# Silu of four input projections: one ScalarE silu each, in pairs, in place of tanh, identity and a VectorE product

## The reference

```python
x_and_res = x @ Wi + bi                       # x: layer-normed input, 128 -> 4 x 128 columns
xs, res = jnp.split(x_and_res, [D_INNER], axis=-1)
xs = jax.nn.silu(xs)
x_dbl = xs @ Wx + bx                          # d_raw, B_sel, C_sel
delta = jax.nn.softplus(d_raw @ Wdt + bdt)
h = exp(delta_t[..., None] * A) * h + delta_t[..., None] * B_t[:, None, :] * x_t[..., None]   # 512 steps
y = C_t * jnp.sum(h, axis=-1)
y = (y + xs * Dp) * jax.nn.silu(res)
out = layernorm(y @ Wo + bo + x)
```

## Time and profile before

| | us |
|---|---|
| median of 3 runs | 2027.9 (2025.98 to 2030.78) |
| the profiled execution: its time | 2027.03 |
| its span, from first to last instruction | 2025.2 |
| DVE busy | 1693.6 (84%) |
| POOL busy | 1519.6 (75%) |
| PE busy | 1377.8 (68%) |
| ACT busy | 1136.7 (56%) |
| mean granted TensorE clock | 0.84 of full speed |

### The profile page before, as it was taken

How to read it: one execution, slowest core, us unless ns; L and a number is a source line. 1 busy time by engine, 2 the same in 40 slices (tenths; PEclk the granted TensorE clock), 3 DMA queues, 4 the chain that set the end, 5 groups by cost and what they waited for, 6 DMA issues and landing times. The chain is left out here.

```text
span 2025.2 us, 23533 instructions
## 1 busy us (share of the span) xinstructions
PE 1377.8 (68%) x5800; PEld 592.7 (29%) x5800; DVE 1693.6 (84%) x2401; ACT 1136.7 (56%) x2176; POOL 1519.6 (75%) x885
## 2 busy tenths in 40 slices
PE   2134448768676878767786768767786768668857
PEld 0000013324232333323332333314332333224424
DVE  1699989999898889898898988998898989896433
ACT  1256755656567555755666655765566656544323
POOL 1198998878987798877987788877987789874111
PEclk9555558879898889878898898879798899879869
DMA  3500320032000400022000310022000310000000
GB/s 90 194 1 0 117 83 0 6 110 81 11 1 25 170 13 0 21 97 77 11 0 24 126 46 11 0 87 108 11 0 24 112 60 6 1 5 1 6 0 6
DMA packets 34153, 88.25 MB, mean 44 GB/s; under 512 B 5363, under 2 KB 20598, under 8 KB 25846
## 3 DMA queue, kind: packets, MB, share of 16 engines
q1 hardware_dynamic: 34038, 87.12, 12.0%
HBM read 75.58 MB, written 11.53 MB: 43 GB/s over the span
## 5 line engine op out<-in xcount | busy, mean ns | idle before, releaser
L815 POOL TENSOR_TENSOR w<-ur,br 128x1024 f32<-128x1024 f32 x512 | 1199.1, 2357 | 237.7 <-DVE h L1114 219.2
L1114 DVE TENSOR_TENSOR_SCAN h<-da,w 128x512 f32<-128x512 f32 x1024 | 1204.4, 1207 | 74.1 <-ACT da L711 28.1
L711 ACT ACTIVATE da<-dr,al 128x511 f32<-128x511 f32 x1024 | 691.1, 692 | 250.1 <-DVE h L1114 225.1
L558 PE MATMUL ys<-h,wsum 128*32 128x512 f32 x2048 | 333.5, 729 | 194.9 <-DVE h L1114 165.9
L499 PE MATMUL bankH<-nT,w 128*128 128x512 f32 x512 | 307.7, 685 | 112.2 <-DVE sq L1044 112.1
L661 ACT ACTIVATE tq<-bankH 128x512 f32<-128x512 f32 x256 | 153.0, 598 | 378.7 <-PE bankH L499 378.7
L499 PE MATMUL bankG<-nT,w 128*128 128x512 f32 x512 | 295.5, 661 | 60.7 <-DVE aq L1053 60.4
L512 PEld LDWEIGHTS bankY<-w,aq 128*128 128x128 f32 x2048 | 263.7, 204 | 114.0 <-issue 64.2
L761 POOL TENSOR_TENSOR x<-x,yk 128x512 f32<-128x512 f32 x128 | 162.5, 1269 | 169.5 <-ACT yk L674 168.8
L512 PE MATMUL bankY<-w,aq 128*128 128x128 f32 x2048 | 270.4, 288 | 27.1 <-DVE aq L1053 19.7
L1044 DVE SCALAR_TENSOR_TENSOR sq<-tq,bankH 128x512 f32<-128x512 f32 x256 | 170.4, 666 | 100.7 <-ACT tq L661 100.5
(11 more groups left out here) (175 smaller groups left out, 837.0 us busy)
## 6 DMA issues: line engine op xcount, KB each, us to landing
br<-b_rows SPq DMA_DIRECT2D x32, 1024.0 KB, 7.8
dr<-d_rows SPq DMA_DIRECT2D x16, 1024.0 KB, 5.3
ur<-u_rows SPq DMA_DIRECT2D x16, 1024.0 KB, 7.9
d_rows<-vh SPq DMA_DIRECT2D x16, 256.0 KB
u_rows<-th SPq DMA_DIRECT2D x16, 256.0 KB
xnew<-in_L_attn_a_x_dram SPq DMA_DIRECT2D x8, 256.0 KB, 3.2
w<-in_L_ffn_W_dram SPq DMA_DIRECT2D x2, 1024.0 KB, 7.0
x<-in_L_attn_a_x_dram SPq DMA_DIRECT2D x8, 256.0 KB, 7.6
```

The lines of the kernel that those rows point to most:

```text
L558: ins = nc.tensor.matmul(ys[32 * q:32 * q + 32, :], wsum[:, :], h[:, (2 * group + q // 2) % H_RING, q % 2, :], start=(n == 0), stop=(n == ...
L711: A(da[duo % D_RING][:, k % 2, 1:L], dr[:, half, q, 1:L], ACT.Exp, scale=nega[:, QUADS * half + q, n:n + 1]).then_inc(decay_ready, 1)
L815: G.tensor_tensor(w[:, duo % W_RING, :, :], ur[:, half, q:q + 2, :], br[:, n:n + 1, :].to_broadcast([128, 2, L]), ALU.mult).then_inc(produ ...
L1114: V.tensor_tensor_scan(h[:, duo % H_RING, k % 2, :], da[duo % D_RING][:, k % 2, :], w[:, duo % W_RING, k % 2, :], 0.0, ALU.mult, ALU.add). ...
```

## The change

ACT writes the silu of a projection straight from the bank, with the bias, into `xs` or `sres`, and frees the bank. Line 622 and DVE's line 970 go, and so does the halving of the bias at the start (line 849). Two projections are taken together: ACT waits for `in0` and `in1` (then for `in2` and `in3`), at the later one's slot plus 3. The waits for the buffers move along: those that guarded `xs` and `sres` on DVE now stand on ACT, and the wait for `steps_stored`, which guarded `th`, stands ahead of line 637. In the table, `in2`, `in3`, `stepsB`, `C0`, `C1` and `dt0` move by one to three slots, and `C0` and `C1` change banks. `copy_out` (line 584) waits for the filled bank, runs one ACTIVATE and frees the bank.

```diff
--- before.py
+++ after.py
@@ -80,8 +80,8 @@
     (S5_AT + 14, "post", "H", "s5"), (S5_AT + 17, "post", "Y", "s5t"),
     (MOE_AT[2] - 2, "post", "Y", "x3T"), (MOE_AT[2], "post", "Y", "lg2"),
 ] + [(PRE_AT + _n, "pre", _b, _name) for _n, _b, _name in (
-    (0, "H", "xnT"), (2, "G", "in0"), (3, "H", "in1"), (6, "G", "in2"), (7, "H", "in3"), (10, "G", "stepsB"),
-    (13, "G", "C0"), (14, "H", "C1"), (16, "G", "dt0"), (24, "H", "dt1"))]
+    (0, "H", "xnT"), (2, "G", "in0"), (3, "H", "in1"), (8, "G", "in2"), (9, "H", "in3"), (12, "G", "stepsB"),
+    (14, "H", "C0"), (15, "G", "C1"), (17, "G", "dt0"), (24, "H", "dt1"))]
 for _m in MOE_AT:
     for _j in range(2 * E):
         PE_STEPS.append((tile_slot(_m, _j), "late" if is_late_tile(_m, _j) else "post", "H", f"h{_m}_{_j}"))
@@ -197,7 +197,7 @@
         ident = sb("ident", [128, 128])
         wsum = sb("wsum", [128, 32])
         rev = sb("rev", [128, E])
-        hbi = sb("hbi", [128, 4]); bxs = sb("bxs", [128, 1]); bxc = sb("bxc", [128, 2])
+        bis = sb("bis", [128, 4]); bxs = sb("bxs", [128, 1]); bxc = sb("bxc", [128, 2])
         bdts = sb("bdts", [128, 2]); dps_ = sb("dps_", [128, 2]); bcs = sb("bcs", [128, 3, D])
         one_col = sb("one_col", [128, 1]); mhalf = sb("mhalf", [128, TT]); minus = sb("minus", [128, TT]); eps = sb("eps", [128, TT])
         al = sb("al", [128, 2 * QUADS, PER_QUAD]); nega = al
@@ -250,7 +250,7 @@
         stats_ready = [sem(f"stats_ready{k}") for k in range(5)]; moments_ready = [sem(f"moments_ready{k}") for k in range(5)]
         rstd_ready = [sem(f"rstd_ready{k}") for k in range(5)]; normed = [sem(f"normed{k}") for k in range(5)]
 
-        tanh_ready = sem("tanh_ready"); biased_ready = sem("biased_ready"); abs_ready = sem("abs_ready"); relu_ready = sem("relu_ready"); exp_ready = sem("exp_ready"); log_ready = sem("log_ready")
+        abs_ready = sem("abs_ready"); relu_ready = sem("relu_ready"); exp_ready = sem("exp_ready"); log_ready = sem("log_ready")
         inputs_ready = sem("inputs_ready")
 
         sums_gated = sem("sums_gated"); scaled_ready = sem("scaled_ready"); x1_ready = sem("x1_ready"); shifted_ready = sem("shifted_ready")
@@ -290,7 +290,7 @@
 
             load(ident[:, :], c_ident)
             load(wi[:, :], Wi)
-            load_columns(hbi, bi, 0, 4)
+            load_columns(bis, bi, 0, 4)
             sp.dma_start(xnew[:, :, :], x[0].rearrange("(a p) c -> p a c", p=128)).then_inc(x_in, 16)
             load(wx[:, :, :], Wx.rearrange("(k p) n -> p k n", p=128))
             load(wdt[:, :], Wdt)
@@ -612,14 +612,15 @@
                 yield SLOT["xnT"] + ACT_LAG
                 copy_out(t, "xnT", xnT[:, :])
                 for m in range(4):
-                    yield SLOT[f"in{m}"] + ACT_LAG
-                    p = got(t, f"in{m}")
-                    if m >= 2:
-                        act.wait_ge(drained[BANK[f"in{m - 2}"]], t.before(f"in{m - 2}") + 1)
-                    elif not known(i, 1):
-                        act.wait_ge(steps_stored[m], 32 * i)
-                    A(th[:, m % 2, :], p[:, :], ACT.Tanh, bias=hbi[:, m:m + 1], scale=0.5).then_inc(tanh_ready, 1)
-                    A(p[:, :], p[:, :], ACT.Identity, bias=hbi[:, m:m + 1], scale=0.5).then_inc(biased_ready, 1)
+                    if m % 2 == 0:
+                        yield SLOT[f"in{m + 1}"] + ACT_LAG
+                        for n in range(m, m + 2):
+                            act.wait_ge(filled[BANK[f"in{n}"]], t.before(f"in{n}") + 1)
+                    if m == 0 and not known(i, 1):
+                        act.wait_ge(gate_ready, 2 * i)
+                        act.wait_ge(direct_ready, 2 * i)
+                        act.wait_ge(inputs_ready, 2 * i)
+                    copy_out(t, f"in{m}", xs[:, m, :] if m < 2 else sres[:, m - 2, :], None, ACT.Silu, bias=bis[:, m:m + 1])
                 yield SLOT["stepsB"] + ACT_LAG
                 if not known(i, 1):
                     act.wait_ge(b_stored, 16 * i)
@@ -633,7 +634,8 @@
                 for m in range(2):
                     yield SLOT[f"dt{m}"] + ACT_LAG
                     p = got(t, f"dt{m}")
-                    act.wait_ge(drained[BANK[f"in{m + 2}"]], t.before(f"in{m + 2}") + 1)
+                    if not known(i, 1):
+                        act.wait_ge(steps_stored[m], 32 * i)
                     A(spa[:, m, :], p[:, :], ACT.Abs, bias=bdts[:, m:m + 1]).then_inc(abs_ready, 1)
                     A(p[:, :], p[:, :], ACT.Relu, bias=bdts[:, m:m + 1]).then_inc(relu_ready, 1)
                 yield SLOT["dt1"] + ACT_LAG + 1
@@ -846,7 +848,6 @@
             chain(V.memset(ones1, 1.0))
             v.sem_inc(ones_ready, 1)
             v.wait_ge(loads, 16 * EARLY_LOADS)
-            chain(V.tensor_scalar(hbi[:, :], hbi[:, :], 0.5, None, ALU.mult))
             for j in range(D_RING):
                 chain(V.memset(da[j][:, :, 0:1], 0.0))
             chain(V.tensor_reduce(wsum[:, :], ident[:, :].rearrange("p (i j) -> p i j", j=QUADS), AX_X, ALU.add))
@@ -958,16 +959,6 @@
                 yield LN_AT[0]
                 v.wait_ge(x_in, 16 * i + 16)
                 yield from moments(0, i, LN_AT[0], xnew)
-                for m in range(4):
-                    yield SLOT[f"in{m}"] + 2
-                    if m == 0 and not known(i, 1):
-                        v.wait_ge(gate_ready, 2 * i)
-                        v.wait_ge(direct_ready, 2 * i)
-                    v.wait_ge(tanh_ready, 4 * i + m + 1)
-                    v.wait_ge(biased_ready, 4 * i + m + 1)
-                    dst = xs[:, m, :] if m < 2 else sres[:, m - 2, :]
-
-                    drain(f"in{m}", V.scalar_tensor_tensor(dst, th[:, m % 2, :], 1.0, banks[BANK[f"in{m}"]][:, :], ALU.add, ALU.mult))
                 for m in range(2):
                     yield SLOT["dt1"] + 6 + m
                     v.wait_ge(relu_ready, 2 * i + m + 1)
```

## The result

The changed kernel takes **2057.16 us** (median of 4 runs, 2054.42 to 2058.37) against 2026.94 (2024.95 to 2030.78) for the kernel before in the same session: ratio **1.0143, 95% interval 1.0131 to 1.0155**. It is 1.4% slower, inside the range of 2028 to 2064, 11 us above the forecast and 1 us above the forecast's own bounds (2038 to 2056). The profiled execution took 2055.97, with a span of 2054.2.

A forecast was written before the change was run, and what follows sets the result against it. DVE was taken to carry the time. Losses of 4.2 (start), 1.2 (batch 0) and 13 (six mixed scans), about 19 us, gave 2046 us, 0.9% slower; own bounds 2038 to 2056, range 2028 to 2064.

The forecast's parts named there:

- The block: ACT, around each pair of projections: two table loads and two silus leave 4.6 us in which no decay is written.
- The rival that rested on a dearer load: ACT: loads into or out of silu's table cost twice Ln's, 41 us more, 2087 us; a drain would act alike; chance 0.03.
- The wait at slot 75: Mixed scans, first pair of silus: DVE stands still 3.9 us for the decay, in place of about 2.1 before.
- `yk` and the statistics: Mixed scan, batch 1: late `yk` moves POOL's sum and DVE's statistics from 393.0 to 394.6, and scan 76 behind them.
- Slot 81 and `nrm`: Mixed scan, second pair of silus: DVE waits below 1 us at slot 81, and `nrm` starts 4.4 us late.
- What PE's order gives back: Mixed scan, from `nrm` to `P1`: fewer products in the path cut the 4.4 us lateness to 2.2 at line 1076.
- A mixed scan: Scans of batches 1 to 6: DVE reaches `P1` 2.2 us late in each, 13 us over six.
- Batch 0: First batch's scan, without statistics: the scan of slot 81 starts at 206.8 instead of 205.6, a loss of 1.2 us.
- The start: ACT's chain ahead of the first scan: +1.7, loads +5.2, second passes gone -2.3, handing to DVE gone -0.4; +4.2 us.
- TensorE's clock falls: Rival: PE idles longer ahead of `stepsB` and `uT` and slows, 2.4 us more in six scans, 2061 us; chance 0.10.
- the ring hiding the blocks: Rival: decay 75 is there in time, so DVE's saved products and waits come out, 2000 us; chance 0.13.
- would be wrong: Stated refutation: DVE's wait at slot 75 below 2 us, or DVE meeting `P1` without waiting.

The follow-up runs named there:

- Experiment 8: Changed kernel with the old slots and banks of `C0` and `C1`, so `C0` stands ahead of the sum again: 2079.15 us, ratio 1.0252.
- experiment 1: Kernel before with only the changed slots and banks of `PE_STEPS`; tanh, halving and product stay: 2040.77 us, ratio 1.0059.
- experiment 2: Changed kernel with Tanh in place of Silu, so without the 32 table loads: 2007.56 us, ratio 0.9904.
- Experiment 4: Changed kernel with a one-column silu ahead of the wait for the first two projections, to load the table earlier: 2032.34 us, ratio 1.0028.
- experiment 6: Changed kernel with first load ahead of the wait, first pair a slot later and ahead of `yk`, second pair a slot earlier: 2036.37 us, ratio 1.0048.
- experiment 10: Kernel before with DVE's products of `in0` and `in1` two slots later and nothing else: 2027.27 us, ratio 1.0004.
- experiment 5: Changed kernel with the pair `in2`, `in3` one slot earlier, so its loads come ahead of decay 80: 2054.05 us, ratio 1.0128.
- experiment 7: As experiment 6, but the first `pre_a`, at the start, keeps the kernel before's tanh, halving and product: 2030.04 us, ratio 1.0018.
- experiment 3: Kernel before plus an unread one-column silu behind the second and fourth tanh of each `pre_a`, 32 loads more: 2065.75 us, ratio 1.0171.

## Why the prediction was right, and where its sizes were off

The mechanism was that of the forecast: blocks of table loads that the ring cannot cover, a late `nrm`, and a wait at `P1`. Three sizes were too small: the start, batch 0 and the mixed scan.

- **The block.** Forecast 4.6 us from T to the next scan, worked out without any silu in the trace (T is the moment at which the second bank is filled): measured 4.59. The load lasts 1.28, the silu begins 0.01 behind it. The drain that the Trainium skill puts beside the load ("ScalarE: Activation LUTs", What ACT_TABLE_LOAD costs) is seen in neither direction: the second silu ends at 401.29, the load begins at 401.31. The rival that rested on a dearer load falls, and with it, for these loads, the page's drain.
- **The wait at slot 75.** Forecast 3.9, in batch 1 4.09, in the six mixed scans 4.46 in the mean and up to 4.90. The forecast took T from batch 1 alone. In batch 3 `in1` takes 1.79 us instead of 1.24, since more of it lies at the lower clock, and ends 3.52 behind slot 72 instead of 2.88.
- **`yk` and the statistics.** Forecast 1.6 late; scan 76 starts 407.67 - 395.78 = 11.89 behind slot 72, before 394.27 - 384.22 = 10.05: 1.8.
- **Slot 81 and `nrm`.** Forecast below 1 us and 4.4 late: 0.88 and 4.7. The wait of 0.92 at slot 82 was not in the sum. It comes because `nrm` (1.63 us) stands on ACT between the decays of slots 81 and 82.
- **What PE's order gives back.** 4.7 late at `nrm`, 2.45 at `P1`: 2.3 back, forecast 2.2. Experiment 8 shows that the order does it, and that without it the loss would have been larger still. What the forecast left out is that the same table costs something too, `stepsB` ahead of `uT` (experiment 1); in the changed kernel `nrm` is so late that this does not show.
- **A mixed scan.** 2.2 forecast; the shift grew by 2.2 to 3.3, in the mean 2.9. Times six that is 17.5 instead of 13: 4 of the 11 us missed. Most of the 0.7 per scan is the wait at slot 75, 0.6 longer than forecast. The statement that DVE waits for next to nothing behind `P1` held (slots 84 to 92 changed by 0.1 in the mean, 0.4 at most).
- **Batch 0.** 1.2 forecast, 2.6 measured. The two blocks cost less than I had summed: the scan of slot 81 is only 0.3 later, not 1.2. But the copy of `C0` then stands on ACT between the decays and waits 2.20 us for PE (rows below), and three scans behind it wait 1.01, 0.43 and 0.50, where DVE ran through before. I had followed `C0` in the mixed scans alone. In the changed kernel's timeline of batch 0:

```profile
218.68 0.69 ACT L586 ACTIVATE cm<-bankH,bxc 128x512 f32<-128x512 f32 x1 [2.20 <-PE bankH L471]
...
219.98 1.22 DVE L1105 TENSOR_TENSOR_SCAN h<-da,w 128x512 f32<-128x512 f32 x1 [1.01 <-ACT da L713]
```

- **The start.** 4.2 forecast, 7.3 measured, the largest miss: 3.1 us. The four loads came as expected, but one of them (line 595) lies in time in which ACT waits for `in3` anyway, and the sum took PE's products as they were, and they are not. The timeline of the changed kernel:

```profile
44.51 1.28 ACT L586 ACT_TABLE_LOAD   x1 [3.96 <-PE bankH L461]
...
46.54 2.08 PE L461 MATMUL bankG<-xnT,wi 128*128 128x512 f32 x2 [2.10 <-ACT xs L586]
...
48.41 1.66 PE L461 MATMUL bankH<-xnT,wi 128*128 128x512 f32 x2
...
52.17 2.91 PE L471 MATMUL bankG<-xs,wx 128*128 128x512 f32 x4 [2.10 <-ACT sres L586]
...
60.06 1.12 PE L478 MATMUL bankG<-steps_and_b,wdt 64*128 64x512 f32 x2 [0.78 <-ACT cm L586]
...
71.61 0.30 DVE L886 TENSOR_TENSOR s5w<-s5w 128x1 f32<-128x1 f32 x1 [1.77 <-ACT s5w L600]
```

  `in2` and `in3` now lie one behind the other with nothing of ACT beside them, 46.54 to 50.07, so that `stepsB` begins 4.15 later (52.17 instead of 48.02). It takes 2.91 instead of 1.98, and PE is done with `C0` and `C1` 4.8 later. Then `dt0`, whose bank G is now that of `C1`, waits 0.78 for the copy: 5.65 later. The load ahead of Exp (line 643) makes it 7.1. Why `stepsB` takes longer, a stretch of the changed kernel's trace (columns as in the earlier trace rows) tells:

```profile
53.20:56.50 3.30, 3.30 (x5) 1.30 (x4) 0.00 (x0) 0.69 (x1) 0.00 (x0) 0.50 0.00 0
```

  From 53.2 to 56.5 the granted clock is at its lower level of 1.2 GHz, and a product takes 0.86 us instead of 0.43. In the kernel before, `stepsB` (48.02 to 50.00) ran at 1.00, and PE's longest idle time in this chain was 0.78; now there are two of 2.10 ahead of the fall. The clock also rises later: before, the pairs `in0` and `in1` took 2.05 and 1.91 us and the pairs from `in2` on 1.13; now `in2` still takes 2.08 and `in3` 1.66. The rival "TensorE's clock falls" was true here, where I had not placed it.
- **The rest.** 0.8 between the stretches and 0.7 behind the last, 1.5 together; I had put nothing there.

7.3 + 2.6 + 17.5 + 1.5 = 28.9. Of DVE's saved work (17.7, forecast 21) and its saved waits (15) nothing came out, as forecast: experiment 2 gives back 19 us of it when the loads are gone. The faster rival, the ring hiding the blocks, was refuted at the point it named: decay 75 wasn't there. But its condition was the right one to name. Experiment 4 took the load ahead of the wait, and 11.8 of the 29 us went by the mechanism alone.

The prediction's "would be wrong" did not come about: the wait at slot 75 is above 2 us, and DVE met `P1` waiting.

## What to carry to other kernels

On an engine that feeds the bottleneck through a short ring, price a function from another table not by its busy time (32 loads, 41 us, on an engine that was idle for 44% of the span) but as a hole in its stream: from the moment its input is there to the next item that the consumer needs, less what the ring holds. Where the engine idles ahead of that input, a one-column call of the function ahead of the wait takes the load out of the hole. And before doing away with an instruction that the bottleneck waits for, try the slot it stands in: here two numbers in the schedule gave 19 us, where removing 32 products by way of silu gave none, but only when both were moved together: a wait taken out of one place of a chain comes back at the next (experiments 6 and 10).

## What the runs showed of the hardware

**The same instructions take 63.1 to 67.8 us.** The slots 92 to 128 of a scan hold the same instructions in all these kernels, and no edit of experiments 1 to 8 touches them. Here batch 3, one stretch from each of four traces (columns as in the earlier trace rows; the number ahead of the two last is the granted clock). Before:

```profile
874.48:940.03 65.55, 46.38 (x199) 19.65 (x200) 57.31 (x82) 40.16 (x71) 50.33 (x28) 0.84 0.37 133
```

The changed kernel:

```profile
895.33:960.85 65.52, 47.78 (x191) 20.31 (x190) 57.27 (x82) 39.93 (x71) 49.82 (x28) 0.79 0.36 133
```

Experiment 1, and experiment 4:

```profile
879.94:947.72 67.78, 49.89 (x198) 21.01 (x199) 57.52 (x83) 40.29 (x71) 50.30 (x28) 0.78 0.35 128
```

```profile
883.38:946.46 63.08, 42.65 (x198) 16.96 (x196) 57.08 (x83) 40.91 (x73) 50.20 (x28) 0.92 0.38 138
```

DVE's work is 57.1 to 57.5 in each, ACT's and POOL's the same within 1 us; of the busy times only PE's differs, 42.65 to 49.89, with a granted clock of 0.92 to 0.78. That is 4.7 us in one scan of eight. But the mean clock alone does not set the time: the first two rows take the same time at 0.84 and 0.79. It matters where in the stretch the lower level lies. At slot 104 stand the first products of a mixture (line 499), whose tanh DVE waits for. Before (PE, then DVE), and then PE in experiment 4:

```profile
892.13 2.05 PE L499 MATMUL bankH<-nT,w 128*128 128x512 f32 x2
...
894.85 0.69 DVE L1044 SCALAR_TENSOR_TENSOR sq<-tq,bankH 128x512 f32<-128x512 f32 x1 [1.60 <-ACT tq L661]
```

```profile
899.49 1.10 PE L499 MATMUL bankH<-nT,w 128*128 128x512 f32 x2
```

In the kernel before the granted clock is at 0.50 from 887.5 to 894.9, the pair takes 2.05 us and DVE waits 1.60. In experiment 4 the clock is back at 1.00 shortly before the pair begins, it takes 1.10 and DVE does not wait. The slots 104 to 107 take 10.27 us before and 8.58 there, 1.7 of the 2.5 us between the two.

Summed over the slots 92 to 128 of batches 1 to 6, for all kernels that keep block 3 in its place (edges at scan starts; the clock is the mean of the six):

| kernel | us | DVE busy | DVE idle | granted clock |
|---|---|---|---|---|
| experiment 1 | 397.9 | 344.8 | 53.1 | 0.794 |
| changed kernel | 389.7 | 343.9 | 45.8 | 0.822 |
| experiment 5 | 389.5 | 344.2 | 45.3 | 0.829 |
| experiment 7 | 388.2 | 344.0 | 44.2 | 0.826 |
| before | 386.3 | 343.8 | 42.5 | 0.842 |
| experiment 2 | 385.2 | 344.1 | 41.1 | 0.841 |
| experiment 6 | 385.2 | 343.5 | 41.7 | 0.838 |
| experiment 8 | 381.7 | 344.5 | 37.2 | 0.860 |
| experiment 3 | 378.9 | 342.9 | 36.0 | 0.840 |
| experiment 10 | 377.3 | 343.3 | 33.9 | 0.875 |
| experiment 4 | 374.4 | 343.0 | 31.4 | 0.902 |

By and large the time falls as the clock rises, over 24 us, nearly as much as the whole change cost (29). Experiment 3 stands out: 7 us less than the kernel before at the same mean clock. This is what came and went "outside" in experiments 1, 4 and 10: 10 is equal to before because 10.2 lost inside met 8.5 won outside and 1.7 behind the last. Which edit turns it which way I could not foretell, and my expectations of experiments 1 and 4 missed by it. In the slots 104 to 107 the path from the clock to DVE's wait is seen; that the clock makes the rest of the 24 us is argued from the table, since no run changed the clock by itself.

**A table load waits with its function.** The load stands directly ahead of the activation that needs it, is held by the waits written ahead of that activation and begins only when those semaphores have come (398.73, 5.04 idle ahead of it), not when ACT falls idle. Its length was 1283 ns in every group of every kernel, for silu's table, the exponential's and Ln's alike.
